# Nystrom attention with a third softmax kernel formed transposed, and remainders of the Newton iteration in halves

## The reference, cut to what matters

```python
Q, K, V = ...                          # 16 heads of 8 features; Q / sqrt(8)
Q_l, K_l = ...                         # 64 landmarks: means over 4 tokens
kernel1 = softmax(Q @ K_l.T)           # 256 x 64 for each head
kernel2 = softmax(Q_l @ K_l.T)         # 64 x 64
kernel3 = softmax(Q_l @ K.T)           # 64 x 256
V = K2.T / max_of_column_sums
for _ in range(6):                     # Newton, for the inverse of kernel2
    KV = K2 @ V
    V = 0.25 * V @ (13*I - KV @ (15*I - KV @ (7*I - KV)))
out = (kernel1 @ V) @ (kernel3 @ values)   # then a projection
```

## Time and profile before

| | |
|---|---|
| three runs, us | 2030.46, 2038.51, 2039.64 (median 2038.51) |
| the profiled execution, us | 2036.87 |
| its span (first to last instruction), us | 2035.1 |
| PE busy | 1849.3 us, 91% of the span |
| DVE busy | 1645.8 us, 81% |
| ACT busy | 1095.1 us, 54% |
| POOL busy | 926.4 us, 46% |
| Nystrom stage, first turn_x to last finish | 888.95 to 1822.86 us |

### The profile page before, as it was taken

One profiled execution on the slowest core, in us unless ns is written; L12 is line 12 of the kernel. 1 busy time (PEld: TensorE's weight loads), 2 busy tenths in 40 slices (PEclk: granted clock), 3 DMA queues, 4 the chain that ended last, 5 costly groups with the idle time before them and its releaser, 6 DMA issues.

```text
span 2035.1 us, 66134 instructions
## 1 busy us (share of the span) xinstructions
PE 1849.3 (91%) x27529; PEld 1415.0 (70%) x27529; DVE 1645.8 (81%) x3980; ACT 1095.1 (54%) x2880; POOL 926.4 (46%) x913
## 2 busy tenths in 40 slices
PE   5998999997999688959999999999999999967887
PEld 4887566665888466647777777777777777744666
DVE  5785999997666699947888888888888888858997
ACT  2444333332444466646666666666666666635664
POOL 2000888884000377724444444444444444426886
PEclk9999999998999899979999999999999999988999
DMA  4000000000000000000000000000000000000001
GB/s 119 1 1 1 1 2 1 2 2 1 1 1 1 0 1 1 1 1 3 3 4 3 3 3 3 4 3 4 3 3 3 4 3 3 3 2 1 21 22 42
DMA packets 14601, 14.44 MB, mean 7 GB/s; under 512 B 1440, under 2 KB 12128, under 8 KB 14304
## 3 DMA queue, kind: packets, MB, share of 16 engines
q1 hardware_dynamic: 11104, 8.83, 1.5%
q10 hardware_dynamic: 3200, 1.37, 0.3%
HBM read 6.01 MB, written 4.19 MB: 5 GB/s over the span
## 4 chain that ended last, share of the span: by engine, by line
PE 62%; DVE 27%; issue 6%; ACT 3%; POOL 1%; DMA 1%; DVEq 0%; POOLq 0%; SPq 0%
PE acc L518 6%; PE acc L495 6%; PE acc L1713 6%; DVE arena L623 5%; PE acc L1703 5%; PE acc L1725 4%; DVE acc L941 2%; DVE arena L954 2%; DVE arena L618 2%; DVE arena L931 2%; PE acc L1755 2%; PE acc L804 2%; PE acc L509 2%; PE acc L1653 2%; DVE arena L1270 2%
## 5 line engine op out<-in xcount | busy, mean ns | idle before, releaser
L1553 POOL TENSOR_TENSOR arena<-arena 128x288 f32<-128x288 f32 (+1 forms) x384 | 292.0, 767 | 459.3 <-ACT arena L1460 400.2
L978 POOL TENSOR_TENSOR arena<-arena 128x960 f32<-128x960 f32 (+2 forms) x74 | 177.6, 2400 | 301.1 <-DVE arena L947 206.0
L1460 ACT ACTIVATE arena<-acc 64x288 f32<-64x288 f32 x384 | 155.4, 405 | 140.8 <-PE acc L1731 133.4
L1279 DVE SCALAR_TENSOR_TENSOR arena<-acc,arena 128x288 f32<-128x288 f32 (+1 forms) x384 | 156.9, 409 | 70.3 <-PE acc L1725 39.4
L726 POOL TENSOR_TENSOR arena<-arena,quadcol 128x512 f32<-128x512 f32 x64 | 79.3, 1257 | 237.8 <-DVE arena L593 237.8
L468 ACT ACTIVATE arena<-acc,wib 128x256 f32<-128x256 f32 x256 | 100.3, 475 | 151.3 <-PE acc L509 151.3
L1064 PE MATMUL acc<-wguT,arena 128*128 128x352 f32 x256 | 105.3, 494 | 48.4 <-DVE arena L931 47.5
L1725 PE MATMUL acc<-arena 64*64 64x72 f32 (+1 forms) x3072 | 135.1, 224 | 11.9 <-DVE arena L1279 11.8
L1713 PE MATMUL acc<-arena 64*64 64x72 f32 (+1 forms) x3072 | 133.1, 223 | 13.7 <-DVE arena L1270 13.4
L1270 DVE SCALAR_TENSOR_TENSOR arena<-arena 128x256 f32<-128x256 f32 x192 | 109.3, 569 | 43.0 <-ACT arena L1460 41.7
L1713 PEld LDWEIGHTS acc<-arena 64*64 64x64 f32 x3072 | 110.9, 133 | 47.0 <-issue 44.9
(11 more groups left out here) (238 smaller groups left out, 4883.7 us busy)
## 6 DMA issues: line engine op xcount, KB each, us to landing
out_dram<-X SPq DMA_DIRECT2D x3, 1024.0 KB, 5.2
out_dram<-X SPq DMA_DIRECT2D x1, 512.0 KB, 3.2
wi<-in_wiT_dram ACTq DMA_DIRECT2D x1, 256.0 KB, 6.1
wout<-in_woT_dram ACTq DMA_DIRECT2D x1, 256.0 KB, 8.0
out_dram<-X SPq DMA_DIRECT2D x1, 256.0 KB, 2.3
out_dram<-X SPq DMA_DIRECT2D x2, 128.0 KB, 2.6
wqkv<-in_w_qkv_dram ACTq DMA_DIRECT2D x1, 192.0 KB, 8.6
arena<-in_w_down_dram SPq DMA_DIRECT2D x1, 176.0 KB, 4.2
```

What stands on the lines that cost most here:

```text
L978: pool.tensor_tensor(b3(y[k][:, part(u)]), b3(z[k][:, part(u)]), each(small[u % kept][:, 1, blocks(u)]), ALU.mult).then_inc(y_ready, 1)
L1279: dve.scalar_tensor_tensor(pm[s][:, group[g], cols], pn[s][:, group[g], cols], part, tm[s][:, group[g], cols], ALU.mult, ALU.add).then_inc ...
L1460: ins = act.mul(sq[s][rows, group[g], :], pn[s][other, group[g], 0:MW], part)
L1553: pool.tensor_tensor(tm[s][:, group[g], cols], pm[s][:, group[g], cols], sq[s][:, group[g], cols], ALU.subtract).then_inc(tm_ready, 1)
```

## The change

In the Nystrom stage:

- **Kernel 3 transposed.** `scores3` is kept for the maxima. `max3` reduces two banks at a time (two calls). PE transposes the maxima (`turn_m3`), DVE puts them into a block of the moving operand (`lower3`), and PE computes the scores a second time, transposed and with the maxima subtracted (`turned3`). ACT then takes two exponentials over 1024 elements. The row sums come out of `start_w`, whose value operand has columns of ones; it has 16 matmuls of 128 columns instead of 8 of 256. The 16 transposes and four copies are gone. ACT prepares a masked copy of the keys (`keys`).
- **Kernel 1** gets its maxima in the same way: two transposes, `lower1` on DVE (two calls), `masked_queries` on ACT, and `turned1` without its 16 small matmuls. POOL forms one more stationary operand (`expand_rows`). Both calls of `turned1` are now in the next pass.
- **Kernel 2**: the maximum goes into the exponentials as bias, eight of 64 columns with accumulator; DVE's subtraction and sum are gone.
- **Group 1's remainder in halves**: DVE reads the swapped square from PSUM, 64 partitions at a time, beside ACT's two activations.
- **The lists** of all four engines are in another order, and what precedes pass 0 has a list of its own, in place of passes -2 and -1.
- Ahead of the first stage: eight more small POOL instructions before `masks`, the four `pick` copies are gone, and the third and fourth loads of x share a semaphore.

```diff
-                    dve.wait_ge(s3_done, n * NQ + q + 1)
-                    dve.tensor_reduce(sm[s][:, NMAX3, 2 * q:2 * q + 2], A[q].rearrange("p (t n) -> p t n", t=2), AX,
+                def max3(n, s, k):
+                    dve.wait_ge(s3_done, n * NQ + 2 * k + 2)
+                    dve.tensor_reduce(m3n[s].rearrange("p o (q t c) -> p (o q) t c", t=2, c=16)[:, 2 * k:2 * k + 2, :, 0],
+                                      psum[:, 2 * k:2 * k + 2, :].rearrange("p q (t n) -> p q t n", t=2), AX,
                                       ALU.max, negate=True).then_inc(max3_ready, 1)
+                def lower3(n, s):
+                    dve.wait_ge(m3T_done, n + 1)
+                    for t in range(2):
+                        ins = dve.scalar_tensor_tensor(mov3[s][:, t, :], mxp[0], pairmask[:, 1 - t:2 - t],
+                                                       qlx[s][:, 2 * t:2 * t + 2, :].rearrange("p h m -> p (h m)"),
+                                                       ALU.mult, ALU.add)
+                    ins.then_inc(mov3_ready, 1)
...
-                def remainder(n, s, it, g):
+                def remainder_half(n, s, it, h):
+                    rows, other = halves[h][0], halves[1 - h][0]
+                    iterate(dve, n, it, 1)
+                    dve.wait_ge(sq_done, step(n, it, 1))
+                    if h == 0:
+                        dve.wait_ge(sq_ready, turn(n, it, 1))
+                    dve.scalar_tensor_tensor(rm[s][rows, group[1], :], pm[s][rows, group[1], 0:LM], 7.0 * size[it],
+                                             pn[s][other, group[1], 0:LM], ALU.mult, ALU.subtract).then_inc(rm_ready, 1)
...
+                def lower1(n, s, t):
+                    dve.wait_ge(mxT_done, n + 1)
+                    dve.wait_ge(qm_ready, n + 1)
+                    dve.scalar_tensor_tensor(mov1[s][:, t, :], A[0][:, 0:SEQ], pairmask[:, 1 - t:2 - t], qm[s][:, t, :],
+                                             ALU.mult, ALU.add).then_inc(mov1_ready, 1)
...
+                def exp2(n, s, k):
+                    act.wait_ge(max2_ready, n + 1)
+                    for p in (2 * k, 2 * k + 1):
+                        act.activation(k2c[s][:, p, :], s2[s][:, p, :], ACT.Exp, bias=sm[s][:, MAX2, p:p + 1],
+                                       accum_out=sm[s][:, SUM2, p:p + 1]).then_inc(e2_ready, 1)
+                def exp3(n, s, k):
+                    act.wait_ge(s3T_done, n + 1)
+                    act.activation(flat(eT[s][:, 4 * k:4 * k + 4, :]),
+                                   psum[:, 2 * k:2 * k + 2, :].rearrange("p q n -> p (q n)"), ACT.Exp)\
+                       .then_inc(e3_ready, 1)
...
+                def square_half(n, s, it, h):
+                    rows, other = halves[h][0], halves[1 - h][0]
+                    act.wait_ge(sq_done, step(n, it, 1))
+                    if h == 1:
+                        act.wait_ge(rm_ready, turn(n, it, 1))
+                    act.mul(sq[s][rows, group[1], :], pn[s][other, group[1], 0:MW], 15.0 / (13.0 * size[it]))\
+                       .then_inc(sq_ready, 1)
...
+                def turned3(n, s):
+                    pe.wait_ge(mov3_ready, n + 1)
+                    pe.wait_ge(kx_ready, n + 1)
                     for t in range(2):
                         for j in range(TPB):
-                            mm = pe.transpose(A[q][:, t * SEQ + j * P:t * SEQ + (j + 1) * P],
-                                              e3[s][:, 2 * q + t, j * P:(j + 1) * P], ident[:, :])
-                    mm.then_inc(e3T_done, 1)
+                            for q in range(NQ):
+                                mm = pe.matmul(A[q][:, t * SEQ + j * P:t * SEQ + (j + 1) * P],
+                                               kx[s][quad(q), t, j * P:(j + 1) * P], mov3[s][quad(q), t, :],
+                                               start=True, stop=True, skip_group_check=True)
+                    mm.then_inc(s3T_done, 1)
...
                     for q in range(NQ):
-                        pe.matmul(A[q][:, t * SEQ:(t + 1) * SEQ],
-                                  klx[buf(n)][quad(q), 2 * t:2 * t + 2, :].rearrange("p h m -> p (h m)"),
-                                  qkT[buf(n)][quad(q), 0, :], start=True, stop=False, skip_group_check=True)
-                    for j in range(TPB):
-                        for q in range(NQ):
-                            mm = pe.matmul(A[q][:, t * SEQ + j * P:t * SEQ + (j + 1) * P], pick[quad(q), j, t, :],
-                                           mxT[s][quad(q), :], start=False, stop=True, skip_group_check=True)
+                        mm = pe.matmul(A[q][:, t * SEQ:(t + 1) * SEQ],
+                                       kst[s][quad(q), 2 - 2 * t:4 - 2 * t, :].rearrange("p h m -> p (h m)"),
+                                       mov1[s][quad(q), t, :], start=True, stop=True, skip_group_check=True)
```

More of the change, by code:

```diff
@@ L1325, in v @@
                 dve.wait_ge(blank, 1)
-                for n in range(-2, NB + 1):
+                landmarks(0, 0)
+                landmarks(1, 1)
+                max2(0, 0)
+                max3(0, 0, 0)
+                max3(0, 0, 1)
+                kernel2(0, 0)
+                lower3(0, 0)
+                columns(0, 0)
+                largest(0, 0)
+                spread(0, 0)
+                begin_w(0, 0)
+                begin_p(0, 0)
+                for n in range(0, NB + 1):
                     s, o = n % STREAMS, 1 - n % STREAMS
@@ L1368, in v @@
                     if run:
+                        remainder_half(n, s, 2, 1)
                         newton(n, s, 2, 0)
+                        remainder_half(n, s, 2, 0)
+                    if tail:
+                        finish(n - 1, o)
+                    if run:
+                        newton(n, s, 2, 1)
+                        remainder(n, s, 3)
                     if head:
@@ L1381, in v @@
                     if run:
-                        newton(n, s, 3, 0)
+                        remainder_half(n, s, 3, 0)
+                    if head:
+                        begin_w(n + 1, o)
+                    if run:
+                        remainder(n, s, 4)
+                        newton(n, s, 3, 1)
                     if head:
@@ new lines, in masked_queries @@
+                def masked_queries(n, s):
+                    act.wait_ge(qk_ready, n + 1)
+                    for t in range(2):
+                        ins = act.activation(qm[s][:, t, :], qkT[buf(n)][:, 0, :], ACT.Copy, scale=pairmask[:, t:t + 1])
+                    ins.then_inc(qm_ready, 1)
+                def exp2(n, s, k):
[3 more added lines that the diff above has]
+                                       accum_out=sm[s][:, SUM2, p:p + 1]).then_inc(e2_ready, 1)
@@ L1475, in a @@
                 act.wait_ge(normed, phase)
-                for n in range(-3, NB + 1):
+                norm(0, 0)
+                norm(1, 1)
+                turned_x(0, 0)
+                turned_x(1, 1)
+                copy_qk(0, 0)
+                copy_qk(1, 1)
+                keys(0, 0)
+                exp2(0, 0, 0)
+                exp2(0, 0, 1)
+                exp2(0, 0, 2)
+                exp2(0, 0, 3)
+                copy_v(0, 0)
+                copy_v(1, 1)
+                turned2(0, 0)
+                exp3(0, 0, 0)
+                exp3(0, 0, 1)
+                turned_kv(0, 0)
+                keys(1, 1)
+                for n in range(0, NB + 1):
                     s, o = n % STREAMS, 1 - n % STREAMS
@@ L1527, in a @@
                     if run:
-                        square(n, s, 5, 0)
-                        turned_mx(n, s)
-                        square(n, s, 5, 1)
+                        square(n, s, 5)
+                        masked_queries(n, s)
+                    if fore:
+                        keys(n + 2, s)
+                    if run:
+                        square_half(n, s, 5, 0)
+                        square_half(n, s, 5, 1)
             def g(pool):
@@ L1584, in g @@
                         remainder(n, s, 4, 0)
+                    if head:
+                        expand_k(n + 1, o)
+                        expand_rows(n + 1, o)
+                    if run:
                         remainder(n, s, 4, 1)
+                        remainder(n, s, 5, 0)
                     if fore:
@@ L1800, in project @@
                     mm.then_inc(y_done, 1)
-                for n in range(-2, NB + 1):
+                turn_x(0, 0)
+                turn_x(1, 1)
+                queries(0, 0)
+                queries(1, 1)
+                scores2(0, 0)
+                scores3(0, 0)
+                values(0, 0)
+                values(1, 1)
+                turn_m3(0, 0)
+                turn2(0, 0)
+                turned3(0, 0)
+                columns(0, 0)
+                start_w(0, 0)
+                factors(0, 0)
+                turn_w(0, 0)
+                start_p(0, 0)
```

(18 more changed lines are left out.)

354 lines of the change are left out of this document (169 added, 185 removed), and 2 rows, old and new, of the table names.

## The result

The changed kernel takes 2017.37 us (median; 2015.19 to 2020.58) against 2036.78 us for the one before on the same chip: a ratio of 0.9908 [0.9894, 0.9921], 19 us or 0.9% faster. The forecast was 1993.5. The sign was right and the time lies inside the whole range (1968 to 2024), but outside the forecast's own (1980 to 2008), and under half of the forecast gain came.

What follows compares the result with a forecast made beforehand. PE was taken as the bound, 98% busy. A pass falls 1.36 us to 26.7, over 31 passes -42; with -2.5 ahead of the loop and -0.5 at the end 1992, stated as 1993.5 (own range 1980-2008, whole 1968-2024).

Steps and rivals of the forecast that it cites:

- PE's work: PE's matmuls and transposes in one pass: priced at -1.83 us, from 27.4 to 25.55 us a pass.
- DVE's work: DVE's instructions in one pass: +1.1 us to 24.6, of which +1.58 for group 1's remainders in twelve halves.
- POOL's stall: Old remainder beside POOL's SBUF reads: about 0.15 us average stall in its 0.571, gone when the halves read PSUM.
- Late place (b): End of the pass: PE's `cross 5` waits 0.4 to 0.5 us for `newton 4,1`, late in DVE's list.
- Late place (a): PE's `turned3` waits about 0.4 us for `lower3`, queued on DVE behind `rh 1,0` and a 0.95 us reciprocal.
- The sum 25.55 + 0.4 + 0.45 + 0.3: Pass length: PE's work plus two late places and small waits at `multiply 3` and `turn_w`, 26.7 us.
- ACT: ACT's work in one pass: net -1.3 of 18.8 us, a third of the pass free, none in the sum.
- Ahead of the loop: From the stage's first transpose to pass 0's first square, 25.95 us before: -2.5 us, between +2 and -5.
- the end: End of the Nystrom stage: -0.5 us for the missing small matmuls.
- the start: Eight more POOL instructions put `masks` about 2 us later, hidden; it would cost only beyond 7 us.
- DVE half-way the bound: Rival, 18%: halves or small instructions cost more than priced, or DVE's waits reach 3 us; pass 27.5, 2018 us.
- The signs of being wrong: Trace limits: DVE busy over 25.5 us a pass, `start_w` 1.3 or more, or PE's gaps over 2.5 us a pass.

## Why the prediction was wrong

- **PE's work**: right, -1.86 for -1.83, and so are its two large terms (`turned3` 1.10, `start_w` 1.01).
- **DVE's work, the step that failed**: "An instruction's time goes by its columns, not by its partitions, if the half costs what the full form from PSUM costs, 0.417". As a duration that was right, 0.420. But the prediction priced PE's groups from start to start and DVE's by duration. In the new row ahead of `cross 5` a half holds the queue for 0.45 us and adds about 0.1 to the one in front of it (0.49 for 0.36, 1.24 for 1.14); the full form holds it for 0.33. DVE's busy time grew by 1.7 us a pass, not 1.1, and undoing the halves takes 2.7 us of it away where the term had +1.58. (The prediction also took 283 us for ten passes; they are 10.09, so DVE's work before was 23.3 us a pass, not 23.5.)
- **POOL's stall**: right for the halves. The 305 halves that the timeline lists singly between 960 and 1790 us all last 0.42 us, beside POOL's difference or not. But the old form would have stalled less too: in the new lists it takes 0.480 us, not 0.571, so the credit was partly the order's. In the row above the half at 1240.75 has this one on POOL beside it:

```profile
1240.86 0.80 POOL L1628 TENSOR_TENSOR arena<-arena 128x288 f32<-128x288 f32 x1 [1.53 <-ACT arena L1507]
```

- **Late place (b)**: the right place and releaser, mis-sized: 0.92 for 0.45. With the old form in iterations 4 and 5 the wait is 0.56; the lost overlap at the two halves of iteration 4 comes to 0.47 by the estimate above, as much as was missing.
- **Late place (a)**: there, at 0.61 for 0.4, but worth nothing. The sum 25.55 + 0.4 + 0.45 + 0.3 added up gaps as if each were time. My reading is that the pass is set by a cycle of DVE's row, `cross 5`, PE's groups after it and DVE's wait for `scores2`. The runs show its part at `cross 5`: 0.59 us out of the row gave 0.60, 0.36 gave 0.36, 0.61 at (a) gave nothing. That the cycle closes through the middle of the pass is argued, not shown.
- **ACT**: outside the bound, though its work fell by 0.4 us a pass and not by 1.3: the eight small exponentials with their accumulator reads take 4.1 us, not 3.1. But the halves tie its second activation to DVE's queue, which the list of effects left out. In the kernel after it waits for DVE's half 23.0 us in ten passes:

```profile
L1507 ACT ACTIVATE arena<-acc 64x288 f32<-64x288 f32 x122 | 49.4, 405 | 47.9 <-PE acc L1827 23.2 <-DVE arena L1282 23.0
```

- **Ahead of the loop, the end, the start**: -2.9 for -2.5, -1.2 for -0.5, hidden as forecast (the DVE instruction of the earlier trace rows starts at 16.75 for 16.56).
- **Rivals**: the second one, "DVE half-way the bound", 2018 with a pass of 27.5, is what happened (2017.4 and 27.57). The runs show its first mechanism, halves that cost more than priced; how much of the miss is theirs alone stays open. Its 18% was too little against 56%.
- **The signs of being wrong** did not sound: DVE's busy time stayed under 25.5 us a pass (25.0), `start_w` under 1.3 (1.01) and PE's gaps under 2.5 (2.04), and still more than half of the gain was missing. They were set too wide.

What stays open: undoing the halves gives back 0.34 us of the missing 0.87 in the mean of ten passes and 0.49 in the commonest pass. The old form brings its own wait for ACT, so the full price of the halves in the new lists is not separated from that wait. Halves that both start at partition 0 in every memory, or other orders of them, were not tried.

## What to carry to other kernels

Price a queue by the distance from start to start, on every engine, and read it from an instruction whose neighbours start at the same partitions; cutting an instruction by partitions more than doubled its queue time here, cutting it by columns added 0.06 us. Look at the commonest pass as well as the mean. When two engines wait for each other in turn, find the wait that sets the pass and count what stands ahead of it; here a gap elsewhere was slack. And when one engine's step is made to wait for another's half, ask what stands in that other queue.

## What the runs showed of the hardware

- DVE starts an instruction some 0.08 us before the one in front has ended (0.33 from start to start for a duration of 0.41). Where it starts at another partition than the last one in that memory it begins only after the end: 0.42 and 0.46 from start to start. Twelve such halves a pass stand in the change.
- Splitting 128x256 with an operand in PSUM: 0.33 us of queue whole, 0.39 as two of 128x128, 0.87 as two of 64x256. Cut by rows the kernel before gets 2.2% slower; cut by columns its time can't be told from before (1.0010 [0.9998, 1.0021]).
- `start_w` with twice the matmuls at half the columns (128 for 256) costs 1.01 us for 1.00.
- An exponential of 128x64 on ACT takes 0.313 us, and the read of its accumulator 0.205 us more.
